# Attention and feed-forward kernel: a forward quarter in a context bank, squares, inverse and guard reductions in other places, weight tiles in every second slot, and the order of one feed-forward slot

## What is computed

```python
corr = irfft(f * conj(f))                       # f = rfft(x)
x = layernorm(x + sum(softmax(top7(corr)) * x shifted by those lags))
sim = softmax(einsum('ncs,nds->ncd', ctx, x) * 256**-0.5, axis=1)
x = layernorm(x + einsum('ncd,nds->ncs', sim, ctx))
x = layernorm(x + x @ W_base.T + _moe_lora(x))
```

## Time and profile before

| what | value |
|---|---|
| median of 3 runs | 2012.11 us (2011.35 to 2013.47) |
| the profiled execution: its own time | 2017.59 us |
| its span | 2015.8 us, with 27865 instructions |
| mean granted TensorE clock | 0.966 |
| TensorE matmul, busy | 1803.6 us (89%) |
| VectorE, busy | 1460.8 us (72%) |
| ScalarE, busy | 798.1 us (40%) |
| GpSimd, busy | 295.8 us (15%) |
| DMA queue of the kernel, share of 16 engines | 86.1% |

### The profile page before, as it was taken

One profiled execution on the slowest core, in us unless ns is written; L12 is line 12 of the kernel. 1 busy time (PEld: TensorE's weight loads), 2 busy tenths in 40 slices (PEclk: granted clock), 3 DMA queues, 4 the chain that ended last, 5 costly groups with the idle time before them and its releaser, 6 DMA issues. The chain is left out here.

```text
span 2015.8 us, 27865 instructions
## 1 busy us (share of the span) xinstructions
PE 1803.6 (89%) x10466; PEld 968.4 (48%) x10466; DVE 1460.8 (72%) x2679; ACT 798.1 (40%) x970; POOL 295.8 (15%) x450
## 2 busy tenths in 40 slices
PE   3898989999963969999999999997599999999997
PEld 2666666666630434445444554443244444444443
DVE  4777787878759867767667767797667767776773
ACT  5777777676635222222222212242322232223221
POOL 3344444535310000000000000000000010001000
PEclk9999999999985989999999999998799999999999
DMA  8899998898749399889998978647999999999993
GB/s 272 214 294 264 294 264 258 230 269 231 211 168 232 100 225 236 198 210 230 239 215 196 221 183 213 159 146 214 220 255 253 262 239 261 255 262 238 266 255 117
DMA packets 648371, 457.06 MB, mean 227 GB/s; under 512 B 590816, under 2 KB 594912, under 8 KB 627424
## 3 DMA queue, kind: packets, MB, share of 16 engines
q1 hardware_dynamic: 648224, 455.15, 86.1%
HBM read 221.78 MB, written 85.98 MB: 153 GB/s over the span
## 5 line engine op out<-in xcount | busy, mean ns | idle before, releaser
L1541 PE MATMUL bank_f<-w_hi_f,a_cols_f 128*128 128x512 f16 x3584 | 1097.5, 383 | 108.6 <-DMA a_cols_f<-rows_f 66.5
L1541 PE MATMUL bank_f<-w_lo_f,a_cols_f 128*128 128x512 f16 x1792 | 686.3, 383 | 0.0
L1541 PEld LDWEIGHTS bank_f<-w_hi_f,a_cols_f 128*128 128x128 f16 x3584 | 353.2, 99 | 545.8 <-issue 53.5
L1541 PEld LDWEIGHTS bank_f<-w_lo_f,a_cols_f 128*128 128x128 f16 x1792 | 176.5, 99 | 204.4 <-issue 6.4
L1134 ACT ACTIVATE rows_f<-xn_f 128x1024 f16<-128x1024 f32 x93 | 98.3, 1057 | 385.1 <-DMA xn_f<-x_scratch 155.2
L1134 ACT ACTIVATE rows_f<-sums_f 128x1024 f16<-128x1024 f32 x93 | 98.0, 1054 | 333.7 <-DMA a_cols_f<-rows_f 326.4
L1309 DVE SCALAR_TENSOR_TENSOR y_f<-bank_f,w_iscale,y_f 128x512 f32<-128x512 f32 x192 | 135.0, 745 | 122.9 <-PE bank_f L1541 89.3
L1270 DVE TENSOR_TENSOR rows_f<-sums_f,rows_f 128x1024 f16<-128x1024 f32 x93 | 113.6, 1221 | 104.9 <-ACT rows_f L1134 104.9
L666 PE MATMUL ps_s_fast<-k_both_fast,q_hi_fast 128*128 128x256 f16 x1024 | 170.0, 274 | 6.2 <-DMA k_both_fast<-v_lo_fast 5.2
L1309 DVE SCALAR_TENSOR_TENSOR y_f<-bank_f,w_iscale_f,y_f 128x512 f32<-128x512 f32 x192 | 134.5, 742 | 42.9 <-PE bank_f L1541 42.8
L524 DVE SCALAR_TENSOR_TENSOR x2buf_fast<-ps_c_fast,iscale_fast,xbuf_fast 128x512 f32<-128x512 f32 x128 | 96.0, 750 | 70.6 <-PE ps_c_fast L655 70.0
(11 more groups left out here) (212 smaller groups left out, 2538.9 us busy)
## 6 DMA issues: line engine op xcount, KB each, us to landing
xbuf_fast<-x SPq DMA_DIRECT2D x32, 1024.0 KB, 6.2
x_scratch<-x2buf_fast SPq DMA_DIRECT2D x32, 1024.0 KB, 6.4
y_f<-x_scratch SPq DMA_DIRECT2D x32, 1024.0 KB, 6.8
xn_f<-x_scratch SPq DMA_DIRECT2D x62, 512.0 KB, 4.7
xn<-x_scratch SPq DMA_DIRECT2D x60, 512.0 KB, 6.0
cbuf<-ctx_in SPq DMA_DIRECT2D x16, 1024.0 KB, 5.8
cbuf_fast<-ctx_in SPq DMA_DIRECT2D x16, 1024.0 KB, 7.0
cbuf<-w_chunks SPq DMA_DIRECT2D x16, 1024.0 KB, 5.5
```

The lines of the kernel that those rows point to most:

```text
L1541: ins = nc.tensor.matmul(bank[i][:], a_cols[:, i, part + kk, :], ww[:, W_SLOT[i], kk, :], start=(kk == 0 and part == 0 and ww is w_hi), st ...
```

## The change

- The fourth forward quarter goes into `ps_c[0]`, a bank of the contexts (`ps_f`); TensorE waits ahead of the quarters for all additions of the slot, and no longer between the third and the fourth.
- The inverse (`guard_inverse`) moves from the end of the slot to the next one, behind the transposed banks 0 to 2; each of these banks now waits for the square that reads it, and the inverse for all four.
- ScalarE takes squares 0 and 1 ahead of `softmax_exp(1)`, squares 2 and 3 behind it.
- VectorE does `guard_lags(0)` behind context addition 1 of the next slot rather than ahead of `softmax_norm(0)`, and `guard_lags(1)` behind addition 3 rather than 0. The verdict of the last slot moves with it.
- The tiles of W go to slots -1, 1, 3, ..., 13, rather than -1 to 6.
- Slot 17 of the feed-forward stage is no longer a late one.

```diff
+        ps_f = ps_t + ps_c[0:1]
...
+        def w_tile_at(n):
+
+            if n == 0 or (n % 2 == 1 and 0 < n < 2 * (W_TILES - 1)):
+                return (n + 1) // 2
+            return None
...
                 def load_weights(n):
-                    if is_batch(n, W_TILES):
-                        after(sp, w_squared, 2 * n)
-                        if isinstance(n, int) and n == 0:
+                    if w_tile_at(n) is not None:
+                        k = w_tile_at(n)
+                        after(sp, w_squared, 2 * k)
+                        if k == 0:
                             sp.dma_start(w_tile[0:ER, :], b_rows).then_inc(w_loaded, 16)
                         else:
-                            sp.dma_start(w_tile[:], w_rows[bass.ds((n - 1) * P, P), :]).then_inc(w_loaded, 16)
+                            sp.dma_start(w_tile[:], w_rows[bass.ds((k - 1) * P, P), :]).then_inc(w_loaded, 16)
...
                     def square_weights(i):
 
-                        if is_batch(n + 2, W_TILES):
+                        if w_tile_at(n + 2) is not None:
+                            k = w_tile_at(n + 2)
                             at = slice(i * HALF, (i + 1) * HALF)
-                            act.wait_ge(w_loaded, 16 * (n + 3))
-                            after(act, w_squared, 2 * (n + 2) + i)
+                            act.wait_ge(w_loaded, 16 * (k + 1))
+                            after(act, w_squared, 2 * k + i)
...
-                            nc.scalar.activation(power[:, m], ps_t[m % 3][:, 0:C], ACT.Square).then_inc(sq_done, 1)
+                            nc.scalar.activation(power[:, m], ps_f[m][:, 0:C], ACT.Square).then_inc(sq_done, 1)
...
                     square_weights(0)
                     square_weights(1)
+                    guard_squares(0)
+                    guard_squares(1)
                     softmax_exp(1)
-                    for m in range(4):
-                        guard_squares(m)
+                    guard_squares(2)
+                    guard_squares(3)
                     normalise1(1)
...
-                        if j == 0:
+                        if j == 1:
+                            guard_lags(0)
+                        if j == 3:
                             guard_lags(1)
-                        if j == 2 and n == nb - 1:
-                            guard_lags(0)
+                        if j == 3 and n == nb - 1:
                             dve.wait_ge(w_squared, 2 * W_TILES)
...
                     x_stats(1)
-                    if n < nb - 1:
-                        guard_lags(0)
                     softmax_norm(0)
...
+                    def guard_inverse(n):
+
+                        pe.wait_ge(sq_done, 4 * (n + 1))
+                        for r in range(R):
+                            if r == 0:
+                                after(pe, g_free[0], n)
+                            else:
+                                pe.wait_ge(exp_done, R * n + 1)
+                            for m in range(4):
+                                ins = nc.tensor.matmul(ps_g[r][:], power[:, m, r * P:(r + 1) * P], inv[:, m, :],
+                                                       start=(m == 0), stop=(m == 3))
+                            ins.then_inc(inv_done, 1)
+
...
                     for p in range(3):
+                        if cur and nxt:
+                            pe.wait_ge(sq_done, 4 * n + p + 1)
                         transposed_bank(p)
+                    if cur:
+                        guard_inverse(n)
...
+                        after(pe, ctx_added, CG * (n + 1))
                         for m in range(4):
-                            if m == 3:
-                                pe.wait_ge(sq_done, 4 * (n + 1) + 1)
                             for k in range(HALF // P):
-                                ins = nc.tensor.matmul(ps_t[m % 3][:, 0:C], fwd[:, k, m * P:(m + 1) * P], u_t[:, k, :],
+                                ins = nc.tensor.matmul(ps_f[m][:, 0:C], fwd[:, k, m * P:(m + 1) * P], u_t[:, k, :],
                                                        start=(k == 0), stop=(k == HALF // P - 1))
                             ins.then_inc(fwd_done, 1)
-
-                        pe.wait_ge(sq_done, 4 * (n + 2))
...
     def late(s):
-        return s in (1, NP_ + 1)
+        return s == 1
```

More of the change, by code:

```diff
@@ L404, in square_weights @@
                                 nc.scalar.activation(w_tile[:, at], w_tile[:, at], ACT.Square,
-                                                     accum_out=w_sumsq[:, bass.ds(2 * (n + 2) + i, 1)]).then_inc(w_squared, 1)
+                                                     accum_out=w_sumsq[:, 2 * k + i:2 * k + i + 1]).then_inc(w_squared, 1)
                     def normalise1(r):
@@ L700, in slot @@
                             pe.wait_ge(tables_loaded, 32)
+                        after(pe, ctx_added, CG * (n + 1))
                         for m in range(4):
-                            if m == 3:
-                                pe.wait_ge(sq_done, 4 * (n + 1) + 1)
                             for k in range(HALF // P):
-                                ins = nc.tensor.matmul(ps_t[m % 3][:, 0:C], fwd[:, k, m * P:(m + 1) * P], u_t[:, k, :],
+                                ins = nc.tensor.matmul(ps_f[m][:, 0:C], fwd[:, k, m * P:(m + 1) * P], u_t[:, k, :],
                                                        start=(k == 0), stop=(k == HALF // P - 1))
                             ins.then_inc(fwd_done, 1)
-                        pe.wait_ge(sq_done, 4 * (n + 2))
-                        for r in range(R):
-                            if r == 0:
-                                after(pe, g_free[0], n + 1)
-                            else:
-                                pe.wait_ge(exp_done, R * (n + 1) + 1)
-                            for m in range(4):
-                                ins = nc.tensor.matmul(ps_g[r][:], power[:, m, r * P:(r + 1) * P], inv[:, m, :],
-                                                       start=(m == 0), stop=(m == 3))
-                            ins.then_inc(inv_done, 1)
                 batch_slots(pe, None, nb, slot, 0)
```

## The result

The changed kernel took 2008.7 us in the median of 14 runs (2006.14 to 2017.12), the kernel before on the same chip 2016.35 (14 runs, 2011.35 to 2022.16): ratio 0.9968, 95% interval [0.9955, 0.9981], or -6.4 us (-9.1 to -3.8). The mean of the three is -9.4, the forecast said -12.1. The profiled execution of the changed kernel was the slowest of its 14 (2017.12 us, span 2015.3), so its end says little against the 2017.59 of before; stages within it can be compared.

A forecast was written before the change was run, and what follows sets the result against it. Attention was taken as bound by a closed loop through the cbuf_fast load, later feed-forward slots by DMA. Terms 3.9 + 1.4 + 1.3 + 5.5 = 12.1 us took 2017.59 to 2005.5, median forecast 2000.0; range 1980 to 2009.

The forecast's parts named there:

- the ring: Attention stage: a closed loop through the cbuf_fast load, ScalarE, TensorE and VectorE sets the slot period, 34.11 us.
- the term of the W tiles: Attention slot 0: with no W tile issued behind the load of cbuf_fast, 1.4 us gained; other end 0.
- no part of V: Attention: W tiles' squares lie on ScalarE between exp 0 and square 0, outside the path to value_low(1)'s end, V.
- Two loops nearly equal, and the change frees only TensorE's: Attention: TensorE's own loop is at most some 0.2 us longer than the context-load loop, which the change hardly touches.
- rival 1: Attention: TensorE's stalls are the whole period; slots go to about 31.8 us, total 1974; chance 0.12. Half, 1985, also 0.12.
- C - V: Attention slot: from value_low(1)'s end (V) until ScalarE can square cbuf_fast (C); 9.97 us, expected to stay about 10.
- Loop 3.9 us: Attention: context-load loop goes from 34.11 to 33.81 us, 0.30 in each of 13 slots; lower bound 0.
- End of attention 1.3 us: Attention slot 14 is TensorE's: 1.8 us won with a W tile ahead, minus some 0.5; range 0 to 2.5.
- The 0.5 for the lags: End of attention: some 0.5 us lost to slot 15's guard lags standing between the last additions.
- Slot 18, 7.8 us earlier: Feed-forward stage: slot 18 starts at about 1442.1, not 1449.91; 5.5 us of it kept in idle DMA time.
- Rival 2: Whole kernel: nothing moves in feed-forward and hardly anything in attention; 2006 to 2012 us; chance 0.18.
- Rival 3: Attention: slower, as the earlier store of x2's second half may delay cbuf_fast's load; at most 2017 us; chance 0.05.

The follow-up runs named there:

- e6: Kernel before with only the load of the context's second half issued ahead of the slot's last key transposition on SyncE (the exchange): 2017.99 us, ratio 0.9995.
- e8: Kernel before plus guard's edits, early slot 18 and the exchange of context load and last key transposition, W tiles one per slot: 1987.73 us, ratio 0.9845.
- e17: Kernel before with slot 18 early and 7/8 of the first output half's store left out in slots 18 to 31: 1996.15 us, ratio 0.9888.
- e4: Kernel before with only the W tiles spread to every second slot: 2020.65 us, ratio 1.0003.
- e7: Changed kernel with the context's second-half load issued ahead of the last key transposition: 1993.17 us, ratio 0.9882 against the kernel before.
- e18: Changed kernel with 7/8 of the first output half's store left out in slots 18 to 31: 1987.24 us, ratio 0.9847 against the kernel before.
- e15: Kernel before plus guard's edits and early slot 18, W tiles one per slot, 7/8 of the first output half's store cut in slots 18 to 31: 1984.33 us, ratio 0.9834.
- e9: The changed kernel again, on another chip: 2009.55 us, ratio 0.9939 against the kernel before.
- e10: Changed kernel with W tiles back to one per slot (guard's edits and early slot 18 stay), second measurement: 2010.02 us, ratio 0.9937 against the kernel before.
- e3: Kernel before with only the guard's edits (fourth quarter, squares, inverse, lags): 2014.04 us, ratio 0.9965.
- e5: Changed kernel with W tiles back to one per slot (guard's edits and early slot 18 stay), first measurement: 2007.75 us, ratio 0.9947 against the kernel before.
- e12: Kernel before with only the guard's edits, measured again on another chip: 2011.17 us, ratio 0.9948.
- e2: Kernel before with only slot 17 no longer late, so slot 18 starts early: 2010.78 us, ratio 0.9956.
- e11: Kernel before with only slot 17 no longer late, second measurement: 2014.68 us, ratio 0.9958.
- e14: Kernel before with only slot 17 no longer late, full stores, third measurement: 2010.32 us, ratio 0.9958.
- e13: Kernel before with only 7/8 of the first output half's store left out in slots 18 to 31: 2002.23 us, ratio 0.9921.
- e16: Kernel before plus guard's edits and the exchange of context load and last key transposition, slot 17 still late, W tiles one per slot: 1987.55 us, ratio 0.9848.
- e1: The changed kernel again, on another chip, for a second profile: 2011.86 us, ratio 0.9952 against the kernel before.

## Why the prediction was right or wrong

The direction and the ring were right; the size was not. Forecast -12.1, measured -6.4, -9.7 and -12.3, -9.4 on the mean. The absolute forecast was 2000.0 us and the result 2008.7: outside the forecast's own range (1993 to 2006) and inside the wide one (1980 to 2009) by 0.3 us, which is luck, as the medians of 2011.86 and 2009.55 on the other chips show.

The step that failed is the term of the W tiles: the prediction put it at a gain of 1.4 us in slot 0, with the tiles' squares at nothing ("no part of V"). The runs show no gain in slot 0, and beside the guard's edits a loss of 3.7 us at the first router product (656.1 against 652.4 with a tile in every slot). A second step, adding the terms in full, failed behind slot 18. Of the forecast 6.6 us were attention and slot 0, 5.5 slot 18; the traces give 3.9 at the first router product, and the medians' 9.4 would leave 5.5 for what follows. That this is just the forecast 5.5 should not be leaned on, since it takes a figure of single traces from one of medians. Point by point:

- **Two loops nearly equal, and the change frees only TensorE's.** Right, and shown from both sides: the exchange alone gives nothing (e6), the guard's edits alone 0.2 to 0.3 us a slot, both together 1.8 (420.11 against 443.47 over 13). The period of e8's later slots, 31.58, is the 31.8 of rival 1, which named the right price for the case that C - V gives way; in the change itself it doesn't.
- **Loop 3.9 us.** Right for the guard's edits: their five profiles with W's tiles one per slot have 440.4 to 442.9 for 13 periods, six of seven without them 443.5 to 445.9 (the seventh, e17, 448.7). The means are 441.3 and, for the six, 444.9: 3.6 us. With the tiles spread as well it is 442.1 to 444.4 in four profiles, mean 443.4: 1.5 us.
- **W tile in slot 0, 1.4 us.** Wrong, and the step that failed: the part costs where I saw a gain. Alone it gives +0.6 us (e4, -1.4 to +2.8). I read the 7.1 us beside 5.7 of the earlier trace rows as what a transfer issued behind the load costs it; with W's tile behind it in slot 0 the load lands after 5.4 to 6.4 us in ten of eleven traces, without after 5.7 to 5.8. The Trainium skill, DMA: Bandwidth & Descriptors, Queues, rings and completion order, says that each DMA engine takes the descriptors of a queue in ring order; by that rule a tile issued behind the load does not slow it, and these traces agree. I also took the tiles' squares to be "no part of V" and so free. Beside the guard's edits the spread takes 3.7 us of the lead at the first router product, and of the time 7.5 us in e7 against e8 (good to 6.7), the only pair that shows a cost in the time; e18 against e15 has 2.6 and e9 against e10 nothing, both within their noise. In part the place is known: in the last slot TensorE's contexts begin 1.97 us after V in the three profiles of the changed kernel and 1.31 to 1.33 in the four with tiles one per slot (e3, e5, e10, e12), and the spread puts a tile's squares right ahead of that slot. The 13 periods are 2.1 us longer as well: 1.4 of it are a later C (C - V 10.27 on the mean of the four profiles against 10.16 of the five), 0.7 the slots at the lower clock shown below. Why the tile lands later isn't settled.
- **End of attention 1.3 us.** Right for attention itself. TensorE's last contexts begin 1.97 us after V in the changed kernel, where e2 and e11 have 3.46 and 3.45: 1.5 us earlier of the 1.8 allowed with a W tile ahead. Without the tile it is 2.1 (1.31) of 2.3. The 0.5 for the lags doesn't show: VectorE starts the last normalisation of x2 48.6 us after the last V in the changed kernel, 50.1 in e2 and e11 and 47.9 in the four with the guard and a tile per slot. But from the last V to the first router product it is 119.4 to 121.2 us in before, e2, e4 and e11, 116.0 to 116.3 in those four with the guard, 116.6 to 118.3 in the changed kernel: some 4 us, or 3 with the spread tiles, which hid part of the step above. The rest of it lies behind attention, in the stretch from that normalisation to the router product (69.3 to 70.6 us without the guard, 68.0 to 69.7 in the changed kernel), and why is open. (In the trace of before another 1.6 us stand at the end: there the last inverse ran at a granted clock of 0.50, and the contexts begin 5.11 us after V.)
- **Slot 18, 7.8 us earlier.** Right: from the first router product to slot 18's LoRA product it is 823.4 us without and 815.4 with the early slot (means of before and e4; of e2, e11, e14), 8.0 us. The 5.5 that I kept of it for the DMA bound is too little for this part alone, which gives 8.6.
- **The sum.** I added the terms as if each were had in full beside the others. They are not: slot 18's 8.6 us alone are 3 beside the guard's (e10 against e12: 2.2; e5 and e10 against e3 and e12: 2.9; each good to 3 or 4) and 0.6 beside the exchange (good to 6). With the store cut the leads at slot 18 come through (e13, e15, e17, e18). "Since the later slots have share 1.01, nothing else can be" won was the right thought, but I applied it to slot 18's gain with nothing ahead of it. Why the part alone escapes the bound better than in company stays open.
- **Rivals.** Rival 2 gave 2006 to 2012, which holds the medians of 2008.7 to 2011.9, but for another reason: slot 18 did start 10 us earlier. Rival 3 didn't come: C - V grew by 0.2 on the mean (10.06 to 10.22), where it decides from 0.9.
- **The execution.** My base was a profiled run 5.5 us above its median. With more runs the kernel before has a median of 2016.35 on this chip and 2018 to 2024 on the others, so only the ratio carries over.

## What to carry to other kernels

When two loops of nearly the same period bind a stage, each fix alone shows little of its worth in that stage (here 0.2 to 0.3 us a slot and nothing) and both together far more than their sum (1.8): measure C - V, find what stands ahead of it in the queue, and exchange that along with the first fix. A stage bound by DMA can take back the lead of an edit that only starts one slot earlier, while one pair of kernels here (e16 and e8) kept the lead of an edit that moves the transfers too: ask of each term which of the two it is before adding them. Where TensorE is busy for less than all of such a stage, cutting one transfer for a test shows within one run what that transfer costs: here 16 us.

## What the runs showed of the hardware

TensorE sometimes comes back from its longer wait before bank 7 at the lower of its two clocks. The changed kernel's windows, columns as in the earlier trace rows, and its timeline at the same place:

```profile
105.50:107.50 2.00, 0.37 (x3) 0.37 (x4) 0.74 (x4) 2.00 (x4) 0.00 (x0) 0.95 1.04 430
107.50:109.50 2.00, 2.00 (x7) 0.97 (x7) 0.69 (x1) 2.00 (x4) 0.00 (x0) 0.50 0.99 418
```
```profile
107.13 0.99 PE L648 MATMUL ps_t_fast<-ident,xbuf_fast 128*128 128x128 f32 x4 [1.92 <-ACT ag_raw L391]
```

In this slot the transposes take 0.99 instead of 0.66 us at a granted clock of 0.50 (1.2 GHz), behind 1.92 us without work, and S - C is 11.26 instead of 10.10. Two of 13 slots have this in the first profile of the changed kernel, one each in e1, e5, e9 and e10, none in e3, e12, e15 and e18: a wait off the path that now and then costs 1.2 us on it. (Without the guard's edits S - C reaches 11.4 too, but at full clock in the slots looked at, of before, e2, e11 and e17.)

Unexpected too was how regular the second half becomes once DMA has room: four kernels, 13 slots each, 496.6 to 497.0 us, where full stores give 509 to 523.
